# The second recurrence's input products move beside attention, into SBUF; read steps take 112 zero columns

## The reference, cut to what matters

```python
xin = einsum('bsd,hd->sbh', x_norm, W_in)
new = tanh(xt + prev @ W_res.T)            # first recurrence, 512 steps,
state = 0.95 * new + 0.05 * prev           # 256 wide, 8 sequences at once
Bm = einsum('bsd,hd->bsh', x_norm, W_B)    # input products of the second
delta = softplus(x_norm @ w_delta + b_delta)
A_bar = exp(A * delta[..., None])
B_bar = Bm * (1.0 - A_bar) / (A + 1e-08)
h = A_bar * prev + B_bar                   # second recurrence, elementwise
```

## Time and profile before

| | |
|---|---|
| median of 3 runs | 617.13 us (614.12 to 618.78) |
| the profiled execution: its time | 613.99 us |
| its span, first to last instruction | 612.1 us |
| mean granted TensorE clock | 0.992 |
| busy: PE, DVE, ACT, POOL | 571.5, 524.4, 430.7, 202.6 us |
| chain that ended last, share by engine | PE 63%, POOL 23%, issue 9%, DVE 2% |

### The profile page before, as it was taken

How to read it: one execution, slowest core, us unless ns; L and a number is a source line. 1 busy time by engine, 2 the same in 40 slices (tenths; PEclk the granted TensorE clock), 3 DMA queues, 4 the chain that set the end, 5 groups by cost and what they waited for, 6 DMA issues and landing times.

```text
span 612.1 us, 29176 instructions
## 1 busy us (share of the span) xinstructions
PE 571.5 (93%) x11514; PEld 469.6 (77%) x11514; DVE 524.4 (86%) x2325; ACT 430.7 (70%) x2258; POOL 202.6 (33%) x426
## 2 busy tenths in 40 slices
PE   6888787999999999999999999999999999999972
PEld 2555454788888888888888888888889988998862
DVE  6789886799888889899989999999767788899985
ACT  5587775477777777777777777777758677777764
POOL 1556464011000001110111111011100599898886
PEclk9999999899999999999999999999999999999997
DMA  6000000000000000000000000000020000000001
GB/s 219 2 2 1 2 2 1 3 4 4 4 3 4 3 4 3 4 4 4 4 4 4 4 3 3 4 3 4 3 73 2 3 20 17 20 16 20 16 19 31
DMA packets 8632, 8.35 MB, mean 14 GB/s; under 512 B 944, under 2 KB 7088, under 8 KB 8496
## 3 DMA queue, kind: packets, MB, share of 16 engines
q1 hardware_dynamic: 8208, 5.51, 3.0%
q10 hardware_dynamic: 288, 0.99, 0.5%
HBM read 3.35 MB, written 2.10 MB: 9 GB/s over the span
## 4 chain that ended last, share of the span: by engine, by line
PE 63%; POOL 23%; issue 9%; DVE 2%; DMA 1%; ACT 1%; POOLq 0%; SPq 0%; DVEq 0%
PE PS L1479 20%; PE PS L1529 15%; POOL prob_lo L448 4%; PE PS L1490 4%; POOL r_dev L516 4%; PE PS L1500 4%; POOL ln_small L526 3%; PE PS L1431 2%; PE PS L1438 2%; PE PS L1432 2%; PE PS L1494 2%; PE PS L1486 2%; POOL k L539 2%; POOL k L502 2%; POOL ln_small L530 2%
## 5 line engine op out<-in xcount | busy, mean ns | idle before, releaser
L637 ACT ACTIVATE y<-PS 128x16 f16<-128x16 f32 x512 | 94.3, 184 | 132.3 <-PE PS L1494 121.4
L1529 PE MATMUL PS<-ballast,ident 128*128 128x245 f16 (+7 forms) x648 | 142.7, 296 | 0.0
L1041 DVE TENSOR_TENSOR y_lo<-ys,y 128x16 f16<-128x16 f32 x512 | 96.5, 188 | 49.1 <-ACT ys L638 38.8
L1479 PE MATMUL PS<-y_lo,res_hi 128*128 128x8 f16 x2048 | 128.0, 168 | 2.3 <-DVE y_lo L1041 1.1
L1479 PE MATMUL PS<-y,res_hi 128*128 128x8 f16 x2048 | 127.4, 168 | 0.2
L1479 PEld LDWEIGHTS PS<-y,res_hi 128*128 128x128 f16 x2048 | 96.8, 96 | 38.8 <-ACT y L637 19.0
L1479 PE MATMUL PS<-y,res_lo 128*128 128x8 f16 x2048 | 123.4, 166 | 0.0
L453 POOL TENSOR_TENSOR small<-small,minus_half 128x2 f32<-128x2 f32 x32 | 25.6, 799 | 295.2 <-DVE y_lo L1041 260.3
L638 ACT ACTIVATE ys<-PS 128x16 f32<-128x16 f32 x512 | 99.1, 194 | 0.0
L640 ACT ACTIVATE kp<-PS 128x16 f32<-128x16 f32 x512 | 97.5, 190 | 0.0
L1479 PEld LDWEIGHTS PS<-y_lo,res_hi 128*128 128x128 f16 x2048 | 87.9, 96 | 5.5 <-DVE y_lo L1041 3.2
(11 more groups left out here) (240 smaller groups left out, 1483.8 us busy)
## 6 DMA issues: line engine op xcount, KB each, us to landing
ys<-in_x SPq DMA_DIRECT2D x8, 256.0 KB, 7.6
out<-gate_all SPq DMA_DIRECT2D x24, 64.0 KB, 1.5
mats<-in_mats ACTq DMA_DIRECT2D x1, 709.0 KB, 5.0
h_last<-h_all SPq DMA_DIRECT2D x4, 128.0 KB, 2.7
gate_last<-gate_all SPq DMA_DIRECT2D x4, 128.0 KB, 2.9
out<-gate_last SPq DMA_DIRECT2D x16, 32.0 KB, 1.9
rows<-in_rows ACTq DMA_DIRECT2D x1, 257.5 KB, 7.5
wall<-in_wall SPq DMA_DIRECT2D x1, 256.0 KB, 4.8
```

Source lines behind the costliest of these rows:

```text
L637: a_.activation(y16[:, :].rearrange("p (m b) -> p m b", m=NH), pre, ACT.Tanh, scale=back).then_inc(y16_ready, 1)
L1041: v.tensor_tensor(y_lo[:, :], ys[:, :, bass.ds(i * STEPS + (1 + t), 1)].rearrange("p n o -> p (n o)"), y16[:, :], ALU.subtract).then_inc(l ...
L1479: t_.matmul(dst[:, m, :], wts[:, k, m * P:m * P + P], st[:, k * B:k * B + B], start=False, stop=False, skip_group_check=True)
L1529: t_.matmul(at[:, 0:size], ident16[:, :], ballast[:, 0:size], start=False, stop=True, skip_group_check=True)
```

## The change

TensorE makes both halves of a tile's input products at once (`drive(j)`, 2 matmuls of 128x128 f32) into the second half of PSUM bank 7, in bodies 4 to 23, in place of the pads at t=6 (tiles 11 to 30), at t=10 (tiles 0 to 10) and at t=15 of body 23 (tile 31). ScalarE copies them, 128x256 at a time, to SBUF (`take_drive`): at t=7 of the same body, at t=2 of the next one, and at t=0 of body 24. `drives_of(j)` gives the place: the tensors that later hold `h_last` and `gate_last` for tiles 0 to 7, a new tensor for 8 to 27, and the used-up weights in `mats` for 28 to 31. TensorE's `feed` is gone from body 24 and the read stage. VectorE's `feed_scaled` and `recur` work in SBUF. SP waits for 16 rows of the second recurrence before it overwrites `h_last`. The zero matmul of 112 columns is now in every body but 24. Line numbers below are those of the hunks' heads.

```diff
@@ -156,8 +156,10 @@
         z_all = sb("z_all", [P, NT])
-        h_last = sb("h_last", [P, B, P])
-        gate_last = sb("gate_last", [P, B, P])
+        last = sb("last", [P, NH, B, P])
+        h_last, gate_last = last[:, 0, :, :], last[:, 1, :, :]
+        drives = sb("drives", [P, NH, 2 * B + B // 2, P])
+        late_drives = mats[:, 0:B * P].rearrange("p (m k n) -> p m k n", m=NH, n=P)
...
@@ -195,6 +197,7 @@
         SPREAD = MISC[:, 288:292]
+        DRIVE = MISC[:, 512 - NH * P:512]
...
@@ -270,7 +273,8 @@
         ssm_zeroed = sem("ssm_zeroed")
-        ssm_fed = sem("ssm_fed")
+        drive_made = sem("drive_made")
+        drive_taken = sem("drive_taken")
         ssm_scaled = sem("ssm_scaled")
...
@@ -337,6 +341,26 @@
         FED_EARLY = STEPS - 4
+        FIRST_DRIVE = 4
+        LATE_DRIVE = FIRST_DRIVE + AHEAD - 2
+
+        def drives_of(j):
+            q, b = j // B, j % B
+            if q == 0:
+                return last[:, :, b, :]
+            if j < NT - B // 2:
+                return drives[:, :, j - B, :]
+            return late_drives[:, :, b - B // 2, :]
+
+        def drive_count(j):
+            return 2 * j + 2 if j < LATE_DRIVE else 2 * (j - LATE_DRIVE) + 1 if j < 2 * LATE_DRIVE else j + 1
+
+        def early_drive(i):
+            return i - FIRST_DRIVE if FIRST_DRIVE <= i < FIRST_DRIVE + LATE_DRIVE else None
+
+        def late_drive(i):
+            j = i + AHEAD - 2
+            return j if LATE_DRIVE <= j < NT - 1 else None
         assert IN_SCAN == SPLIT
...
@@ -382,6 +406,7 @@
             sp.wait_ge(h_ready, NT)
+            sp.wait_ge(ssm_done, B * NH + EIGHT_FREE)
             for half in range(2):
...
@@ -686,11 +711,19 @@
             act.reg_load(keep_scale, setup[0:1, 24:25].bitcast(I32))
+            def take_drive(j):
+                act.wait_ge(drive_made, drive_count(j))
+                a_.activation(drives_of(j), DRIVE.rearrange("p (m n) -> p m n", m=NH), ACT.Copy).then_inc(drive_taken, 1)
+
             for i in range(FIRST_DECAY):
...
                         gate_half(i)
+                    if t == 2 and early_drive(i - 1) is not None:
+                        take_drive(early_drive(i - 1))
+                    if t == 7 and late_drive(i) is not None:
+                        take_drive(late_drive(i))
                     if (t, i) == (7, 17):
...
@@ -745,6 +778,8 @@
                 scan(t, FIRST_DECAY, FIRST_DECAY % REGIONS)
+                if t == 0:
+                    take_drive(NT - 1)
                 if t >= 2:
...
@@ -1258,6 +1293,9 @@
+            def drive_row(s, c):
+                return drives_of(half_q(c) * B + c % 2 * 4 + s % 4)[:, s // 4, :]
+
             def feed(s, c):
...
@@ -1266,8 +1304,8 @@
             def feed_scaled(s, c):
-                dve.wait_ge(ssm_fed, c * 8 + s + 1)
-                fed = PS[:, 6 + s % 2, 0:P]
+                dve.wait_ge(drive_taken, drive_count(half_q(c) * B + c % 2 * 4 + s % 4))
+                fed = drive_row(s, c)
                 if half_q(c) == NQ - 1:
...
@@ -1278,15 +1316,16 @@
                 dve.wait_ge(ssm_done, n - 7 + EIGHT_FREE)
+                fed = drive_row(s, c)
                 first = ssm[:, m, half_q(c), (c % 2) * 4 * P + k * P + P - 1:(c % 2) * 4 * P + k * P + P]
                 if half_q(c) == NQ - 1:
-                    v.tensor_tensor_scan(row[:, 0, :], row[:, 0, :], PS[:, 6 + s % 2, 0:HALF], first, ALU.mult, ALU.add
+                    v.tensor_tensor_scan(row[:, 0, :], row[:, 0, :], fed[:, 0:HALF], first, ALU.mult, ALU.add
                                          ).then_inc(ssm_halved, 1)
                     dve.wait_ge(ssm_halved, n - 8 * 2 * (NQ - 1) + 1)
-                    v.tensor_tensor_scan(row[:, 1, :], row[:, 1, :], PS[:, 6 + s % 2, HALF:P], row[:, 0, HALF - 1:HALF], ALU.mult, ALU.add
+                    v.tensor_tensor_scan(row[:, 1, :], row[:, 1, :], fed[:, HALF:P], row[:, 0, HALF - 1:HALF], ALU.mult, ALU.add
                                          ).then_inc(ssm_done, 1)
                 else:
-                    v.tensor_tensor_scan(row, row, PS[:, 6 + s % 2, 0:P], first, ALU.mult, ALU.add).then_inc(ssm_done, 1)
+                    v.tensor_tensor_scan(row, row, fed, first, ALU.mult, ALU.add).then_inc(ssm_done, 1)
...
@@ -1485,7 +1524,7 @@
                           skip_group_check=True)
-                zeros = 112 if i < FIRST_DECAY else 0
+                zeros = 112 if i != FIRST_DECAY else 0
                 if zeros:
...
@@ -1528,8 +1567,31 @@
+            def drive(j):
+                b, q = j % B, j // B
+                pe.wait_ge(b_t_ready, 1)
+                if drive_count(j) > 1:
+                    pe.wait_ge(drive_taken, drive_count(j) - 1)
+                pe.wait_ge(xn_ready, j + 1)
+                for m in range(NH):
+                    one = t_.matmul(DRIVE[:, m * P:m * P + P], b_t[:, m * P:m * P + P], xn[:, b, 1 + q * P:1 + q * P + P],
+                                    start=True, stop=True, skip_group_check=True)
+                one.then_inc(drive_made, 1)
+
             def pads(t, i):
                 j = i + AHEAD
+                if t == 6 and late_drive(i) is not None:
+                    pe.wait_ge(gate_raw, late_drive(i) + 1)
+                    drive(late_drive(i))
+                    return
+                if t == 10 and early_drive(i) is not None:
+                    pe.wait_ge(gate_raw, j - 1)
+                    drive(early_drive(i))
+                    return
+                if t == 15 and j == NT:
+                    pe.wait_ge(gate_raw, NT)
+                    drive(NT - 1)
+                    return
                 tile, early, fill_at = j < NT, j <= NT, i % REGIONS < 2 and t in (4, 5, 8, 9)
...
@@ -1552,6 +1614,8 @@
                         pe.wait_ge(gate_raw, j - 1)
+                        if late_drive(i) is not None:
+                            pe.wait_ge(drive_taken, drive_count(late_drive(i)))
                         for n in range(2 if fill_at else 4):
...
@@ -1663,13 +1727,6 @@
-            def feed(s, c):
-                m, k = s // 4, s % 4
-                pe.wait_ge(ssm_done, c * 8 + (s - 1) + EIGHT_FREE)
-                t_.matmul(PS[:, 6 + s % 2, 0:P], b_t[:, m * P:m * P + P],
-                          xn[:, (c % 2) * 4 + k, 1 + half_q(c) * P:1 + half_q(c) * P + P],
-                          start=True, stop=True).then_inc(ssm_fed, 1)
-
             def spread_delta(n):
...
@@ -1722,7 +1779,6 @@
             pe.wait_ge(pv_done, NA * NT)
-            pe.wait_ge(b_t_ready, 1)
             pe.sem_inc(k_cols_free, 1)
...
@@ -1731,8 +1787,6 @@
                 spread_delta(2 * t + 1)
-                if t >= 4:
-                    feed((t - 4) % 8, (t - 4) // 8)
             for i in range(FIRST_READ, BODIES):
...
@@ -1743,9 +1797,6 @@
                         pe.wait_ge(decayed, 2 * 2 * NQ)
-                    f = FED_EARLY + (i - FIRST_READ) * 8 + t // 2
-                    if t % 2 == 0 and f < 8 * 2 * NQ:
-                        feed(f % 8, f // 8)
                     body_readouts(readout, t, i)
...
```

## The result

The changed kernel takes 641.62 us (median of 6 runs, 637.98 to 642.11), against 614.58 us (median of 6, 613.78 to 618.78) for the kernel before on the same chip. The ratio is 1.0408, 95% interval 1.0366 to 1.045: 4% slower, where +5.3 us, less than 1%, had been forecast, and outside the range. The profiled execution took 642.04 us, its span is 640.2, and its mean granted TensorE clock 0.903 instead of 0.992. I read that last number first, because it says where to look. All ratios here leave out executions that took over 1.5% more than the fastest of the same kernel.

What follows compares the result with a forecast made beforehand. GpSimd's chain was taken to bound the read stage, TensorE being busy nearly throughout the decay body. The terms -2.4 - 0.5 + 1.2 + 0.2 + 6.8 = +5.3 us, on the 617.13 us median, gave 622.4; range 610 to 631.

Steps and rivals of the forecast that it cites:

- rival D: Read stage: TensorE's clock falls to 1.2 GHz since products go, up to +35 us, over 650; chance 0.04.
- Part 3: Products replacing pads beside attention: +1.2 us for 20 steps at t=6, 0 at t=10 and t=15.
- Part 1: Decay body: 12 of its 16 steps lose their product, 0.20 us each, -2.4 us.
- Part 2: First read body: 8 products go (-0.8 us), zero columns cost +0.3, net -0.5.
- Part 4: ScalarE's 32 copies of 128x256 to SBUF: +0.2 us in all.
- rival C: Attention: ScalarE's copies at t=7 delay tanh, forecast + 2.0 us, 624.4; chance 0.05.
- Part 5: SP's copies into h_last wait for 16 recurrences, some 8 us into the first read body: 0.
- Part 6: Read stage: VectorE's scan and product with two SBUF inputs hold up GpSimd, 0.31 us a group, 22 groups, +6.8 us.
- Rival B: Read stage: VectorE-GpSimd lock held for whole instructions, 0.67 us a group, +13.2 us in all, 630.3; chance 0.24.
- rival A: Read stage: lock absorbed, TensorE's relief shows, groups fall to GpSimd's 4.11 us, -5.7 us in all, 611.4; chance 0.20.

Runs made afterwards that it cites:

- e9: Kernel before with the read stage's input products cut from 128 columns to 8, nothing else: 646.46 us against 614.61, ratio 1.0514.
- e3: Changed kernel plus one matmul of 512 zero columns in each read-stage place that had a product: 623.64 us against 615.08, ratio 1.0143.
- e1: Changed kernel with VectorE back on PSUM, TensorE's feed back, no read-stage zeros; copies made but unread: 622.23 us against 615.08, ratio 1.0125.
- e2: e1 with VectorE's operands in SBUF; TensorE still makes the products, which nobody reads: 626.04 us against 615.08, ratio 1.018.
- e4: Changed kernel without the 112 zero columns in the read steps: 634.7 us against 615.08, ratio 1.0294.
- e14: Changed kernel with one wait instead of four ahead of each product beside attention, plus e3's zero matmuls: 621.03 us against 616.06, ratio 1.0069.
- e13: Kernel before with only the decay body's 12 products moved beside attention, plus 384 zero columns in odd steps of bodies 26 to 31: 614.09 us, ratio 0.9964.

## Why the prediction was wrong

**The step that failed is the dismissal of rival D.** The prediction named the mechanism ("the clock falls to 1.2 GHz in the read stage, since products go"), gave it 0.04, and argued against it with one row: "581.4 to 589.7 has none and kept 1.00". That row is 8.3 us long. The changed kernel issues no input product from body 24 on, and it kept 1.00 for 41 us before the clock fell at 499.4, 8 us into body 26:

```profile
458.20:499.40 41.20, 39.40 (x732) 36.30 (x732) 33.10 (x155) 31.15 (x171) 12.99 (x31) 1.00 0.12 30
```

In e9, whose products are short from body 25 on, the clock fell 23 us behind the start of that body. So even 41 us at 1.00 told nothing of what came next. A row further on in the kernel before would have warned me:

```profile
589.70:605.20 15.50, 8.61 (x63) 6.74 (x61) 13.95 (x64) 10.48 (x45) 13.24 (x35) 1.00 0.10 23
605.20:612.10 6.90, 0.00 (x0) 0.00 (x0) 1.77 (x8) 1.83 (x4) 3.15 (x11) 0.50 0.16 35
```

Behind the last step TensorE works for 8.61 of 15.50 us and is still granted 1.00; the fall comes only at 605.2. A short stretch at 1.00 shows that the clock hasn't fallen yet, and nothing about what it would do over the 110 us of bodies 26 to 31. The Trainium skill (TensorE: Matmul & The Clock Gate, section "Part 1: The HAM clock gate") says that a monitor sets the clock by how busy the array has been; e3 and e9 agree, as only zero columns and missing columns decide there. The price was mis-sized too. It was "up to +35", from 0.4 us a step for which no row was given; the changed kernel paid 17.4 in bodies 26 to 31 (e3 against it). At the low clock its even and odd steps took 1.34 and 1.27 us, where they had taken 1.10 and 1.05 in the kernel before (means over bodies 26 to 30).

**Part 3 was mis-sized.** Forecast +1.2, measured +7.2 in the profiled pair and 7.3 in e1. Counting weight loads was right for t=10, as the equal 0.44 us show. Left out were the semaphore waits ahead of the product, 0.13 us a step for three of them, and the f32 end behind it, 0.09. By the table of section 3 that is 20 x 0.25 at t=6 and 11 x 0.19 at t=10, 7.1 us; the one at t=15, also put at 0, cost 0.14. The 0 for the 11 at t=10 was the weakest line. I had counted ScalarE's wait and the one at t=8, and none that TensorE merely passes. The f32 end could have been read in the trace of the kernel before, in its decay body, where a product stands right ahead of a step:

```profile
455.61 0.30 PEld L1669 LDWEIGHTS PS<-xn,b_t 128*128 128x128 f32 x2
455.83 0.26 PEld L1479 LDWEIGHTS PS<-y,res_hi 128*128 128x128 f16 x4
456.02 0.17 PEld L1479 LDWEIGHTS PS<-y,res_lo 128*128 128x128 f16 x4
```

From 455.83 to 456.02 it is the same 0.19.

**Part 1 was right**: -2.4 forecast and measured. In the changed kernel's decay body the steps take 0.90 us, or 1.10 where a fill (L1539) stands between two of them; the kernel before had 1.11 and 1.33 in the same places. Both show in its tanh starts:

```profile
461.46 0.18 ACT L662 ACTIVATE y<-PS 128x16 f16<-128x16 f32 x1 [0.18 <-PE PS L1533]
...
462.36 0.18 ACT L662 ACTIVATE y<-PS 128x16 f16<-128x16 f32 x1
...
463.47 0.18 ACT L662 ACTIVATE y<-PS 128x16 f16<-128x16 f32 x1 [0.20 <-PE PS L1533]
```

**Part 2**: -0.5 forecast, -0.1 measured. Body 25 takes 17.36 us in e1, 17.48 in e2, 16.93 in e4 and 17.26 in the changed kernel. So VectorE's operands cost 0.12 there, which the sum had left out; the products' absence brought 0.55 instead of 0.8, and the zeros cost 0.33, as forecast (+0.3).

**Part 4 and rival C**: +0.2 forecast, nothing measured. The copy at t=7 was expected about 0.5 us into its step, with an end just where the next tanh wants ScalarE. It starts 0.21 us into the step in all 20 bodies, takes 0.40 us, less than the 0.48 of the earlier trace rows, and ScalarE then waits 0.29 us for TensorE, as in body 20:

```profile
406.98 0.18 ACT L662 ACTIVATE y<-PS 128x16 f16<-128x16 f32 x1 [0.29 <-PE PS L1533]
...
407.19 0.40 ACT L716 ACTIVATE drives<-PS 128x256 f32<-128x256 f32 x1
407.88 0.18 ACT L662 ACTIVATE y<-PS 128x16 f16<-128x16 f32 x1 [0.29 <-PE PS L1533]
```

The product holds up this step's own tanh too, and so it is done by the time ScalarE comes to the copy.

**Part 5**: SP's later wait shows nowhere: e1 has it, and its bodies 25 to 31 take as long as before.

**Part 6 was right that VectorE and GpSimd would wait for each other, and near in size, in part by luck.** 0.31 us a group forecast, 0.25 measured (e2), +4.7 (e3) to +5.8 (e2, with a clock dip in it) instead of +6.8. Its two terms were the wrong way round: 0.28 for the scan and 0.11 for the product, where the rows below show GpSimd losing 0.11 to the scan and 0.15 to the product. Rival B's 0.67, by whole durations, is refuted, and rival A's 0 as well. The timeline of e3 shows one group from both sides:

```profile
514.33 0.45 POOL L565 TENSOR_TENSOR k<-k,h_all 128x128 f32<-128x128 f32 x1
514.33 0.73 DVE L1328 TENSOR_TENSOR_SCAN keep<-keep,drives 128x128 f32<-128x128 f32 x1
...
514.74 0.57 POOL L527 TENSOR_TENSOR k<-k,gate_all 128x128 f32<-128x128 f32 x1
...
514.98 0.36 DVE L1076 TENSOR_TENSOR y_lo<-ys,y 128x16 f16<-128x16 f32 x1
...
515.39 0.61 POOL L531 TENSOR_TENSOR h_all<-k 128x128 f32<-128x128 f32 x1
...
515.41 0.28 DVE L1311 SCALAR_TENSOR_TENSOR drives<-keep,drives 128x128 f32<-128x128 f32 x1
```

The scan and L565 start together. L565 takes its usual 0.45 us, and the scan 0.73 instead of 0.46, so it ends 0.28 behind L565. L527, which starts at 514.74 while the scan is still at work, takes 0.57 instead of 0.46 and ends 0.25 behind the scan. The product keeps its 0.28, and L531 takes 0.61 and ends 0.31 behind it. So each time the one that waits ends only after the other, by less than its own length, and what it loses is less than the other's duration. The rule of the Trainium skill that the prediction quoted (SBUF — State Buffer, "SBUF: two separate sides") is that whoever starts first has the port for its whole instruction and the other waits. That the waiting one ends behind the other agrees with it; what fails is rival B's step from there to the price, the whole duration. By the starts in these rows the first doesn't always win: L531 starts 0.02 us ahead of the product and is the one that waits.

With the clock held and three of the waits gone, e14 comes near the sum: 4.2 us by the ratio and 6.6 by its stretches, where +5.3 had been forecast. That is partly luck, as its terms had moved both ways: +3.1 instead of +1.4 beside attention, +5.5 instead of +6.8 in bodies 26 to 31.

## What to carry to other kernels

When work leaves TensorE in a stage that another engine bounds, look at the granted clock before anything else: the work may have been worth its place for the clock it kept, and zero columns that wait for nobody (e3, e13) give that back. A short stretch that kept the full clock is no evidence for a long one. Price an inserted matmul by its weight loads, and add the semaphore waits ahead of it even if all are met long before, and the later start of f16 weights behind f32 products, wherever TensorE doesn't wait for another engine anyway.
